# First-batch projections every four slots, bias and weight preparation inside attention, output chunks by halves in two sets, in an attention layer on one core

## The reference, cut to what matters

```python
B, C, E, H = 4, 2048, 256, 16            # head size 16
def attn(x, Wq, Wk, Wv, Wo, bo):
    q, k, v = heads(x @ Wq), heads(x @ Wk), heads(x @ Wv)
    scores = where(causal, q @ k.T, -inf)
    ctx = softmax(scores / sqrt(E)) @ v
    return merge(ctx) @ Wo + bo
def ffn(x, weight, bias):                # both operands quantised by blocks of 32
    xq, xs = mx_quantize(x)              # scale = max|block| / 7.5, nearest of the FP6 E2M3 grid
    wq, ws = mx_quantize(weight)
    return (xq * xs) @ (wq * ws).T + bias
x = x + attn(layernorm(x), Wq, Wk, Wv, Wo, bo)
x = x + ffn(layernorm(x), weight, bias)
```

## Time and profile before

| | |
|---|---|
| Median of three runs (lowest to highest) | 2210.75 us (2209.54 to 2210.94) |
| The profiled execution | 2213.29 us |
| Its span, first to last instruction | 2211.6 us |
| Busy in the span: PE, DVE, ACT, POOL | 2067.0, 1671.3, 1342.8, 790.3 us |
| Mean granted TensorE clock | 0.978 |

### The profile page before, as it was taken

One profiled execution on the slowest core, in us unless ns is written; L12 is line 12 of the kernel. 1 busy time (PEld: TensorE's weight loads), 2 busy tenths in 40 slices (PEclk: granted clock), 3 DMA queues, 4 the chain that ended last, 5 costly groups with the idle time before them and its releaser, 6 DMA issues.

```text
span 2211.6 us, 36629 instructions
## 1 busy us (share of the span) xinstructions
PE 2067.0 (93%) x13061; PEld 861.3 (39%) x13061; DVE 1671.3 (76%) x3026; ACT 1342.8 (61%) x2881; POOL 790.3 (36%) x1077
## 2 busy tenths in 40 slices
PE   2789999999999999999999999999999999999973
PEld 1334343343334343443434344343434333343432
DVE  5587777868886868787697877777888888888754
ACT  1136666667665657666675766656676666666640
POOL 4313233241333525334433443535232232323232
PEclk8899999999999999999999999999999999999986
DMA  2341130404031141402213141131303030210111
GB/s 92 120 126 51 48 97 28 109 28 107 6 90 32 57 106 38 125 31 59 85 42 83 45 109 47 47 107 39 108 4 104 4 101 7 71 37 6 51 41 41
DMA packets 180753, 139.79 MB, mean 63 GB/s; under 512 B 56406, under 2 KB 180572, under 8 KB 180572
## 3 DMA queue, kind: packets, MB, share of 16 engines
q1 hardware_dynamic: 180572, 137.45, 22.7%
HBM read 85.73 MB, written 50.86 MB: 62 GB/s over the span
## 4 chain that ended last, share of the span: by engine, by line
PE 81%; DVE 9%; issue 2%; ACT 2%; SPq 2%; POOL 2%; DMA 1%; POOLq 0%; ACTq 0%; DVEq 0%
PE psum L1226 22%; PE psum L1209 22%; PE psum L1191 18%; PE psum L1268 7%; PE psum L1261 5%; DVE max_parts L947 4%; PE psum L1196 2%; PE psum L1251 2%; PE psum L1244 1%; SPq L543 1%; DVE out_shop L1114 1%; DMA shop<-in_L_attn_x 1%; ACT probs L805 1%; PE psum L1290 1%; ACT acc_sb L812 1%
## 5 line engine op out<-in xcount | busy, mean ns | idle before, releaser
L947 DVE TENSOR_REDUCE max_parts<-psum 128x1 f32<-128x512 f32 (+3 forms) x2240 | 1380.1, 667 | 403.4 <-PE psum L1196 210.2
L805 ACT ACTIVATE probs<-psum 128x512 f32<-128x512 f32 (+3 forms) x2560 | 1231.1, 538 | 694.9 <-PE psum L1209 687.4
L1191 PE MATMUL psum<-k_rows,q_rows 96*128 96x512 bf16 (+3 forms) x2560 | 839.3, 349 | 23.8 <-DVE max_parts L947 16.6
L1209 PE MATMUL psum<-q_rows,k_rows 99*128 99x512 bf16 (+3 forms) x2560 | 854.3, 351 | 2.6 <-ACT probs L805 1.9
L1226 PE MATMUL psum<-probs,v_in 128*17 128x512 f32 (+3 forms) x5120 | 594.3, 536 | 10.4 <-ACT acc_sb L812 8.3
L1209 PEld LDWEIGHTS psum<-q_rows,k_rows 99*128 99x128 bf16 x2560 | 237.1, 97 | 621.2 <-ACT probs L805 463.6
L645 POOL TENSOR_SCALAR_AFFINE_SELECT probs<-probs 128x512 f32<-128x512 f32 x256 | 165.0, 645 | 854.2 <-ACT probs L805 854.1
L1191 PEld LDWEIGHTS psum<-k_rows,q_rows 96*128 96x128 bf16 x2560 | 250.6, 98 | 223.5 <-DVE max_parts L947 80.7
L1196 PE MATMUL psum<-maskb,identb 128*128 128x128 bf16 x1024 | 198.7, 220 | 0.0
L1226 PEld LDWEIGHTS psum<-probs,v_in 128*17 128x17 f32 x5120 | 86.1, 95 | 216.7 <-issue 145.8
L1196 PEld LDWEIGHTS psum<-maskb,identb 128*128 128x128 bf16 x1024 | 101.1, 99 | 68.8 <-issue 0.7
(11 more groups left out here) (116 smaller groups left out, 1353.8 us busy)
## 6 DMA issues: line engine op xcount, KB each, us to landing
qk_scratch<-shop SPq DMA_DIRECT2D x64, 384.0 KB, 2.9
q_rows<-qk_scratch SPq DMA_DIRECT2D x384, 64.0 KB, 2.4
k_rows<-qk_scratch SPq DMA_DIRECT2D x384, 64.0 KB, 2.4
shop<-in_L_attn_x SPq DMA_DIRECT2D x18, 512.0 KB, 4.4
v_scratch<-shop SPq DMA_DIRECT2D x16, 544.0 KB, 3.8
v_in<-v_scratch SPq DMA_DIRECT2D x64, 136.0 KB, 2.4
ctx_scratch<-ctx_out SPq DMA_DIRECT2D x64, 128.0 KB, 1.7
out_shop<-ctx_scratch SPq DMA_DIRECT2D x56, 128.0 KB, 3.1
```

Source lines behind the costliest of these rows:

```text
L805: nc.scalar.activation(probs[s % NPROBS][:, h, a:CHUNK], bank[SCORE_BANKS[n % 3]][:, a:CHUNK], ACT.Exp, scale=SCALE).then_inc(probs_ready, 1)
L947: nc.vector.tensor_reduce(max_parts[k % 2][:, first:first + heads, t % TILES, c], ring_bank(UNIT_USE[n])[:, 0:heads * width] .rearrange("p ...
L1191: ins = nc.tensor.matmul(dst[:, i * width:(i + 1) * width], q_rows[u][0:ROWS, qc, first + i, t % TILES * P:(t % TILES + 1) * P], k_rows[u] ...
L1209: nc.tensor.matmul(bank[SCORE_BANKS[n % 3]][:, a:CHUNK], k_rows[u][0:ROWS + LEVELS, h, kb * P:(kb + 1) * P], q_rows[u][0:ROWS + LEVELS, qc ...
```

## The change

The first batch's chunks start every four slots (PRO is 20, `place_early`), and their x is loaded four slots ahead. ACT writes the bf16 part of their q and k projections beside the float32 copy, in place of DVE's cast. ACT also writes the rows of ones: the first buffer's ahead of the slots, the second's in slots -8 to -5. Loads of w_o, w_f and the biases move behind the load of x of chunk 4, on a semaphore of their own; bias work moves to slots 34 to 40, weight work to slots 46 to 53, with buffers of the output as scratch. Output work is placed and done by halves of two tiles, from the transposes to the store; each half's transposes fill one PSUM bank and are copied by one ACT instruction. Two sets of buffers are used from chunk 8 on. For chunks 12 to 15 only three head groups are read from DRAM; the last group's context goes from DVE straight into the tile that is transposed, and dequantising is on DVE.

```diff
-PRO = 19
+PRO = 20
-        return max(0, min(4, 2 * (p + PRO - 10))) + max(0, min(8, 2 * (p + PRO - 13)))
+        return max(0, min(4, 2 * (p + PRO - 11))) + max(0, min(8, 2 * (p + PRO - 15)))
+def place_early(n):
+    start = -PRO + 4 * n
+    sync(-PRO if n < 2 else start - 4, "load_x", n)
+    for a in range(2):
+        vector(start + 1, 0.85, "stats", n, a)
+    vector(start + 1, 0.65, "moments", n)
+    pool(start + 1, 1.0, "deviation", n)
+    for a in range(2):
+        vector(start + 2, 1.0, "quick_normal", n, a)
+    for e in range(EH):
+        item(start + 3, 0.45, "turn_x", n, e)
+    for m, p in ((0, start + 4), (1, start + 4), (2, start + 5), (3, start + 6)):
+        r = 4 * n + m
+        item(p, 1.75, "project", n, m)
+        vector(p + 1, 0.7, "quick_split", r)
+        pool(p + 1, 1.8, "split_low", r)
+        sync(p + 2, "store_qk", r)
+    item(start + 5, 1.75, "project_v", n, 0)
+    item(start + 7, 1.75, "project_v", n, 1)
+    sync(start + 9, "store_v", n)
+    return start + 9
...
-vector(-PRO + 4, 3.0, "weights", 0)
-vector(-PRO + 6, 3.0, "weights", 1)
-item(-PRO + 10, 0.5, "turn_weights")
+for i in range(2):
+    for part in range(2):
+        vector(34 + 4 * i + 2 * part, 2.0, "bias", i, part)
+p = 46
+for step in range(6):
+    p = vector(p, 1.4, "weights", step)
+item(p + 1, 0.5, "turn_weights")
...
-    return n % 2 if late(n) else 0
+    return n % 2 if n >= NCH - 2 * QC else 0
...
-            for u in range(2):
-                nc.gpsimd.memset(k_rows[u][ROWS:ROWS + LEVELS, :, :], 1.0).then_inc(rows_of_ones, 1)
-                pool.wait_ge(rows_of_ones, u + 1)
+            def ones_rows(u, h):
+                nc.scalar.copy(k_rows[u][ROWS:ROWS + LEVELS, h, :].rearrange("p (a n) -> p a n", n=P),
+                               onesb[ROWS:ROWS + LEVELS, None, :].broadcast_to([LEVELS, C // P, P])
+                               ).then_inc(rows_of_ones, 1)
...
+                if early(n):
+                    wait(act, qk_stored[r % 2], 16 * (r // 2))
+                    nc.scalar.copy(parts[r % 2][:, 0, :], ring_bank(ITEM_USE["project", n, m]))
                 nc.scalar.copy(proj[r % 2], ring_bank(ITEM_USE["project", n, m])).then_inc(scalar_emptied, 1)
...
-                wait(dve, qk_stored[v], 16 * (r // 2))
-                link(nc.vector.tensor_copy(parts[v][:, 0, :], proj[v]))
...
+                if k < NK - QC:
+                    wait(dve, ctx_stored[k % 2], 16 * (k // 2))
+                    normal_ctx = ctx_out[k % 2][:, :, :, :]
+                else:
+                    n = NCH - NK + k
+                    dve.wait_ge(for_scalar, ITEM_NO["turn_ctx", before_in_set(n)[0], 1])
+                    normal_ctx = ctx_in[out_set(n)][:, :, E - HG * D:E].rearrange("p j (h d) -> p j h d", h=HG)
...
+            def turn_half(use, t, a):
+                emptied(pe, use)
+                for e in range(EH):
+                    for j in range(2):
+                        ins = nc.tensor.transpose(ring_bank(use)[:, (2 * e + j) * P:(2 * e + j + 1) * P],
+                                                  t[:, 2 * a + j, e * P:(e + 1) * P], ident[:, :])
+                ins.then_inc(for_scalar, 1)
```

More of the change, by code:

```diff
@@ L186, in place_project, with in_order, place_output @@
         if j is not None:
-            p = item(p + gap, 1.75, "project_v", n, j)
-        p += gap
+            p = item(p + 1, 1.75, "project_v", n, j)
+        p += 1
     sync(max(p, q) + 1, "store_v", n)
     return max(p, q) + 1
-def place_output(n, start):
+STAGE = {}
+def in_order(stage, p):
+    return max(p, STAGE.get(stage, p))
+def place_output(n, a, p):
     quick = late(n)
     gap = 0 if quick else 1
[L196 to L241, removed]
-    return p + 2
@@ L246, with out_set, before_in_set @@
+    spend("vector", p + 1, 0.7)
+    sync(p + 2, "store_out", n, a)
+    return p + 2
+def out_set(n):
+    return n % 2 if n >= NCH - 2 * QC else 0
+def before_in_set(n):
+    same = [m for m in range(n) if out_set(m) == out_set(n)]
+    return (same[-1] if same else None), len(same)
+TURNED = {}
 for k in range(NK):
@@ L269 @@
         k = (QC * (b + 1) - 1) * QC + c
[L270 to L276, removed]
+        before, times = before_in_set(n)
+        free = 0
+        if before is not None:
+            free = DONE_AT[before] + 1
+        elif out_set(n):
+            free = max(PROJECTED.values()) + 2
+        if late(n):
+            load = max(TURNED[k - QC] + 4, READ_AT[before] + 2)
+            ready = max(TURNED[k] + 1, load + 2)
+        else:
+            load = max(TURNED[k] + 4, free)
+            ready = load + 2
+        sync(load, "load_ctx", n)
+        sync(max(load, free), "load_again", n)
+        ready = max(ready, free)
+        ends = [place_output(n, a, ready) for a in range(2)]
+        READ_AT[n], DONE_AT[n] = STAGE["turn_ctx"], ends[-1]
 for g in range(NG):
@@ L321, with ctx_groups @@
                 USES.append(("vector", n_vector))
[L324 to L332 removed]
+def ctx_groups(n):
+    return H // HG - late(n)
 def layer_kernel(nc, x, wq, wk, wv, wo, bo, wf, bf, out):
@@ new lines, in split_bias, with place_bias @@
+            def split_bias(i):
+                L = slice(0, LEVELS)
+                b = bias_in[i][L, :]
+                dve.wait_ge(later_loaded, N_LATER)
+                link(nc.vector.tensor_copy(bias_part[L, 0, :], b))
+                for l in range(1, LEVELS):
+                    link(nc.vector.tensor_tensor(out=b, in0=b, in1=bias_part[L, l - 1, :], op=ALU.subtract))
+                    link(nc.vector.tensor_copy(bias_part[L, l, :], b))
+            def place_bias(i):
+                L = slice(0, LEVELS)
+                b = bias_in[i][L, :]
@@ L919, in scale_weights @@
+                for l in range(1, LEVELS):
+                    link(nc.vector.tensor_scalar(b, bias_part[L, l, :], ident[L, l:l + 1], None, ALU.mult))
+                    link(nc.vector.tensor_tensor(out=bias_sum[L, :], in0=bias_sum[L, :], in1=b, op=ALU.add))
+                nc.vector.tensor_copy(bias_rows[i][L, :], bias_sum[L, :]).then_inc(bias_ready, 1)
+                dve.wait_ge(bias_ready, i + 1)
             def scale_weights():
                 t3 = wf_flat.rearrange("p (a b) -> p a b", b=BLOCK)
-                amax, scale, inv = block_max[0][:, 0:WB], block_scale[0][:, 0:WB], inv_scale[0][:, 0:WB]
+                dve.wait_ge(later_loaded, N_LATER)
@@ L941, in round_weights, with weights_work @@
                                         op=ALU.mult).then_inc(wf_ready, 1)
+            def weights_work(p):
+                for i, part in at("bias", p):
+                    if part == 0:
+                        split_bias(i)
+                    else:
+                        place_bias(i)
+                for step, in at("weights", p):
+                    if step == 0:
+                        scale_weights()
+                    elif step == 1:
+                        divide_weights()
+                    elif step == 2:
+                        shift_weights()
+                    elif step == 3:
+                        round_weights(w_even, w_lo)
+                    elif step == 4:
+                        round_weights(w_odd, w_hi)
+                    else:
+                        dequantise_weights()
@@ L1029, in moments_of2 @@
                 if before is not None:
-                    dve.wait_ge(xn2_ready, 2 * before + 2)
-                for j in range(TILES):
+                    dve.wait_ge(xn2_ready, 2 * before + a + 1)
+                for j in (2 * a, 2 * a + 1):
                     ins = nc.vector.bn_aggr(moments2[w][:, j, :], stats2[w][:, j, :])
```

344 lines of the change are left out of this document (187 added, 157 removed).

## The result

The changed kernel takes 2191.33 us (median of 4 runs, 2187.58 to 2193.98) against 2210.85 us beside it (2209.54 to 2213.48): a ratio of 0.9909, 95% interval 0.9892 to 0.9926. It is 19.5 us faster. The direction was right, the size was not: 2169 us had been forecast, and 2191 lies above the range. The profiled execution took 1.8 us more than its span of 2192.2. Of the executions of all experiments one, of 2375.23 us at a mean granted clock of 0.842, was in a slower state and is left out of every figure.

The account below looks back on a forecast made before the run. PE bounds the middle, so gains lie at the ends: -30.5 + 2 + 5 + 0 + 5.2 + 5 - 28.3 = -41.6 us of span, 2211.6 to 2170.0, giving a median of 2169 us (own range 2158 to 2181, chance 0.60).

Parts of the forecast that it names:

- Opening, -30.5: Up to the first exponential: 39.0 us of holes go, +6.5 new wait, +2 low clock; -30.5 us, at 97.5.
- The 9.3 us of the fill: Opening, first chunk: the fill of ones leaves POOL, so its power starts 9.3 us earlier.
- The hole of 21.5 us goes: Opening, before the third chunk's transposes: PE's 21.5 us wait disappears when bias and weight work leaves.
- x of chunk 4, +2 (0 to 9): Start of attention: chunk 4's x, asked for behind a row load, lands later; +2 us, bounds 0 to 9.
- Moved work, +5 (0 to 18.9): Slots 34 to 54: of 18.9 us bias and weight work on DVE, 5.2 don't fit its idle time; +5 us.
- without idle: Sign in attention: DVE has no idle time in slots 34 to 54, where the moved work stands.
- Rival C: Moved work shows in full, with POOL's ops at the wide weight ops: +22 us, 2191 us; chance 0.05.
- Output 0 to 11 by halves, 0 (-3 to +12): Attention, output chunks 0 to 11: DVE's and POOL's extra small ops are covered by idle time; 0 us.
- Rival D: Output by halves: DVE's queue holds units behind small ops waiting for POOL, every chunk; slower, 2229 us; chance 0.03.
- The last groups: End of attention: a feed and eight transposes enter, +5.2 us; PE and DVE wait for each other, +5, bounds 0 to 20.1.
- Rival B: End of attention is set by DVE's chain: +20 us instead of +5, 2184 us; chance 0.12.
- Tail, -28.3: After the last values matmul: last add at T + 37.0 instead of T + 64.8, smaller last store; -28.3 us (-31 to -22).

Follow-up runs that it names:

- three slots with the work: Changed kernel with its first four chunks three slots apart instead of four, and the bias and weight work back in the opening: 2183.60 us, ratio 0.9874.
- three slots without: Changed kernel with its first four chunks three slots apart instead of four, bias and weight work still in attention: 2179.15 us, ratio 0.9855.
- the kernel that has the work back: Changed kernel with the bias and weight work put back into the opening, all else as changed: 2193.25 us, ratio 0.9919.
- the run with the slot between: Changed kernel with transposes of dequantised halves one slot behind the dequantise step, chunks 12 to 14, not in the same slot: 2173.39 us, ratio 0.9829.
- the kernel with only the last half moved: Changed kernel with only the transposes and feed of chunk 14's second half moved behind the last attention slot: 2186.57 us, ratio 0.9890.

## Why the prediction missed

Its sum was 41.6 us of span, and the spans differ by 19.4. Step by step:

- **Opening, -30.5:** -27.3 at the first exponential; six profiles whose opening is the same code lie between 100.44 and 103.44, so single figures here are good to some 3 us. The size was near, by luck, and the make-up wrong. The 9.3 us of the fill came as written (ACT's copies of ones 7.29 us, 7.4 forecast). "The hole of 21.5 us goes" credited the bias and weight work with all of it; taking the work back costs 12.6. The new order was given +6.5 for one wait at 62.5 to 69 and +2 for the low clock. The profile has a wait of 4.91 us ending at 65.20, for POOL's maxima, and one of 4.36 ending at 89.72, for ACT's copy, and no wait of PE over 1 us for loaded rows in 62 to 70. Four slots in place of three cost 5.8 us, and 11.9 at accumulator 1; that three would be faster was not seen, since the stagger had no price of its own. The other edits of the opening gave 21.3 us together (PE no longer waits for all weights, x loaded a chunk ahead, the fill), of which I had 17.5. Along the chain of profiles before, three slots with the work, three slots without, changed kernel, that is -21.3 - 11.8 + 5.8 = -27.3, against -17.5 - 21.5 + 8.5 = -30.5: 9.7 us too much for the work, 3.8 too little for the rest, and 2.7 too much for the new waits.
- **x of chunk 4, +2 (0 to 9):** +4.2 in the changed kernel, inside its bounds. DVE waited 6.13 us, eight units of 4.88 us stood behind, and PE waited 7.06 for those: a wait of one load grew on its way.
- **Moved work, +5 (0 to 18.9):** +8.5 (from accumulator 1 to 6), and 8.5 less in the kernel that has the work back. Over the whole stretch DVE was not full (busy 108.2 of 126.8 us), but it was where the work stood (28.2 of 29 us at the weight steps), as the sign "without idle" had it. Fitting the work by the idle sum of 250 to 300 us asked only whether DVE had room in total. Spread, it costs 4. Rival C (22 us, POOL and DVE taking turns at the weights) is refuted: the seven wide two-input operations took 6.7 us together, three of them 1.1 to 1.5 us, so 1.9 over seven times 0.69 and not the 8.2 that it counts.
- **Output 0 to 11 by halves, 0 (-3 to +12):** from accumulator 12 to 60 the changed kernel and its variants are 2.0 us longer than before on the mean of 13 profiles (-0.3 to +5.4). Rival D, 3.8 us a chunk, is refuted. That stretch also took in chunk 11's feed, which stood behind accumulator 60 before.
- **The last groups, +5.2 for the work and +5 for "PE and DVE, nearly equal and waiting for each other":** this is the step that failed. The late stretch grew by 21.7. The added work is not in it, since chunk 11's feed left as chunk 14's came (96 attend and feed matmuls in both kernels). It is 14.0 us more of PE's idle time and 7.8 us of the same matmuls at a lower clock. I had reckoned DVE as 61 of 65 us full, 53 of them busy, and took the two engines' loads for the cost. But DVE was busy 92.5 of 136 us, and 35.7 of the last 65. What cost was the order: PE's slot ended on DVE's dequantise step (17.6 us of waits, 1.2 before), while DVE's own slot already hung on PE's at the adds before the change (22.7 us there, 25.7 after). One slot of distance gives 20.8 of the 21.7 us back. Rival B had the place and came near the size (+20 for +5). I also read over the slot of distance that the diff takes away. Rival B's reason, DVE full, is refuted by the run with the slot between, where the same DVE work fits into 115.4 us. The clock in the late slots had no term at all.
- **Tail, -28.3:** -28.4. The last add ends 37.3 us after the last values matmul, 37.0 forecast.

By size, the sum of the errors is 3.2 + 2.2 + 3.5 + 3.4 + 11.5 - 0.1 = 23.7 us in this profile (3.4 is the middle of accumulators 6 to 60, where 0 was forecast), against 41.6 - 19.4 = 22.2; the 1.5 between them were gained from the first exponential to accumulator 0. Of the signs named beforehand, the first exponential (92 to 104) and PE's longest hole (under 8) came as written. The time from the first exponential to the last values grew by 36 us, above the 30 named as what would make the forecast wrong.

What stays open is how the 7.8 us of slower matmuls divide between PE's waits, one by one, and why exactly four slots cost PE 4 us in 60 to 80 us: ACT's waits for the stores at the cast (29.6 us, 22.2 with three slots) go with it, but moving the cast changed nothing.

## What to carry to other kernels

Where two in-order engines share a schedule of slots, look at the edges between them and not only at each one's load: if A's slot ends on B's and B's next hangs on A's, both wait though neither is full. Here one slot of distance on one edge gave 20.8 us in a stretch of 136 and cost 1.0 in the tail. A hole that ends on an engine's work need not close by as much as it is long when that work moves (here some 12 of 21.5 us); take the work back alone before crediting it. Place moved work by the slots that it fills, thin, and not by the idle sum of a stretch.

## What the runs showed of the hardware

PE's granted clock was lost in the middle of dense work, not only at the ends. With six waits of 2.0 to 3.6 us within 80 us the late stretch had a clock of 0.91 in place of 0.99 (a mean over parts at 2.4 and parts at 1.2 GHz), which made the same matmuls 7.8 us longer (a score pair 1.06 us after a wait of 3.57, 0.60 before it; values matmuls of 512 columns 682 ns on the mean after 619). With the waits mostly gone it was 0.99 again, with 5.3 us of them left. So here 14.0 us more of waiting went with 7.8 us of slower work, about half a microsecond for each. The length of a single wait did not settle it: the clock fell around five of the six waits and not at that of 1.96 us, and in the kernel with only the last half moved not after those of 2.2 and 2.85 us either. In the kernel with the slot between it fell after a wait of 1.53 us and not after those of 1.60 and 1.92.
